# Edge pass of a graph layer: the aggregated row made in one operation, or in two of 512 and 256 columns

## The chip, the cores and the metric

The kernel runs on one core of a Trainium2 chip. A core has five engines with a queue of their own each: TensorE (PE; its weight loads are listed as PEld), VectorE (DVE), ScalarE (ACT), GpSimd (POOL) and SyncE (SP, which here only starts transfers). They are kept in step by semaphores alone: an instruction names a semaphore and the count that it waits for, and another raises the count when it is done. The metric is device time in microseconds, the median of several runs.

## The reference, cut to what matters

A graph attention layer over 50,000 nodes of 768 features and 25,000 edges, followed by a small feed-forward layer:

```python
hv = layernorm(x).reshape(n, 12, 64)
ft = einsum('nhd,od->nho', hv, W)
e  = leaky_relu(a1[src] + a2[dst], 0.2)          # a1, a2: one number per node and head
alpha = segment_softmax(e, dst)
msg = alpha[:, :, None] * ft[src]
agg = segment_sum(msg, dst)
x   = x + relu(agg + einsum('nhd,od->nho', hv, W_res))
x   = x + ffn(layernorm(x))                      # 768 -> 96 -> 768, other weights for six rows
```

The edges are sorted by target node, and everything is fp32.

## The kernel before, in words

The kernel has two passes. The **edge pass** goes over the edges in 196 chunks of 128 (an edge to a partition), and writes for each chunk the sums of its messages by target, 128 rows of 768 columns, to a scratch in memory. The **node pass** goes over the 392 tiles of 128 nodes, gathers those sums and does the rest. The change is in the edge pass alone.

The edge pass is a software pipeline written out by hand. One loop body holds 14 steps, and in each step every engine works on chunks of several ages: a stage that lags the gather by L steps handles chunk c - L in step c. Steps 0 to 27 and the drain are written out; the rest is a hardware loop. Seven chunks make a group: the softmax over the targets, and the small vectors of mean and variance, are worked out once in a group. Each engine's order is the order of the code; nothing moves an instruction.

What matters here, by line. VectorE, in the order of one step:

- L1196 `nm_s`, once in seven steps: the mean times the reciprocal deviation of a group of source rows. ScalarE's L736, which normalizes those rows, waits for it.
- L1213: copies 13 numbers per partition (`a2_all`) that TensorE's small matmul L967 made; not in four of fourteen steps (`OFF_PE`).
- L1231, **the aggregated row**: adds to the masked sum, which TensorE left in PSUM (`sum_ps`, 768 columns in two banks), a rank-one correction (`csr` times a number per partition, `nmd`), and writes the row to one of seven buffers, `agg_ring`. It raises `s_eo`.
- L1249: the messages of a later chunk (768 columns), then L1099 (two statistics of 384 columns each), L1306 (the 0/1 mask of a chunk) and, in some steps, L1330, L1339 and the chain of the softmax (L1312 to L1382).

TensorE, in a step: transposes L904, feature products L913, the small products L941, then the **masked sum** of a chunk: L955 (columns 0 to 511) and L957 (columns 512 to 767) with the mask as weights, and after it L967. An fp32 matmul shows as two loads and two matmuls in the trace. There is one `sum_ps`, so the sum of a chunk may overwrite it only when the row of the chunk before has been made: this is the wait for `s_eo` ahead of L955. In the drain two places take turns (`twice`).

ScalarE, in a step: L736 (normalizes), L762 (copies the transposes out of PSUM), L768 (copies the features), L773 (copies the small products; TensorE's L967 waits for it) and L781 (squares). SyncE starts the store of a row (L515) when `s_eo` has reached its count. VectorE's `nmd` (L1348) and TensorE's work after the pass wait for `s_eo` too.

Of the kernel before, what the change touches and what calls it, by code (L numbers as in the profile page):

```python
# [14 lines left out]
P = 128  # L15
NC = D // P
# [10 lines left out]
G = 7  # L27
BODY = 2 * G
EC = -(-N_EDGES // (P * BODY)) * BODY
# [17 lines left out]
AR = 7  # L47
# [80 lines left out]
def at_least(eng, sem, value):  # L128

    if not isinstance(value, int) or value > 0:  # L130
        eng.wait_ge(sem, value)


def gnn_ffn_kernel(nc, x, x_cols, edges, dst_rows, dst_next, dst_prev, dst_ends, chunk_base, sel_heads,
# [4 lines left out]
    ALU = mybir.AluOpType  # L139
# [4 lines left out]
    with ExitStack() as ctx:  # L144
# [88 lines left out]
        csr = sb("csr", [P, P])  # L233
# [19 lines left out]
        nmd = sb("nmd", [P, 2, G])  # L253
# [40 lines left out]
        with ExitStack() as edge:  # L294
            agg_ring = edge.enter_context(nc.sbuf_tensor("agg_ring", [P, AR, D], f32))
# [7 lines left out]
        def sums(b, co):  # L303

            return sum2_ps if isinstance(b, int) and co > EC - L_SUM + L_FT and (EC - 1 - co) % 2 == 1 else sum_ps

        def twice(b, co):

            return 1 if isinstance(b, int) and co > EC - L_SUM + L_FT + 1 else 0
# [81 lines left out]
        s_eo = sem("s_eo")  # L391
# [73 lines left out]
        def _(sp):  # L465
# [37 lines left out]
            for b in turns(sp, NB, 2):  # L503
                for i in range(BODY):
                    for h, (at, lo, hi) in enumerate(((19, 0, 4), (22, 4, G))):
                        gl = 2 * b + (i - at) // G
                        if (i - at) % G == 0 and exists(gl, NG):
                            at_least(sp, s_mask, G * (gl - 1) + hi)
                            sp.dma_start(dst_all[:, lo * P:hi * P], dst_rows[ds(gl, 1), lo * P:hi * P].to_broadcast([P, (hi - lo) * P]))\
                                .then_inc(d_dst[h], 16)  # L510
                    co_ = BODY * b + i - L_AGG
                    if exists(co_, EC):
                        v = (i - L_AGG) % AR
                        sp.wait_ge(s_eo, co_ + 1)
                        sp.dma_start(agg_v[ds(co_, 1)].rearrange("a p d -> p (a d)"), agg_ring[:, v, :])\  # L515
                            .then_inc(d_agg[v], 16)
                    if isinstance(b, int) and co_ == EC - 12:
                        sp.wait_ge(s_a2c, EC)
                        sp.wait_ge(s_sqd, EC)
                        sp.wait_ge(s_tr, NBLK * EC)  # L520
                        sp.wait_ge(s_ag, EC)
                        sp.dma_start(sel_sb, sel_heads).then_inc(l_fix, 16)
                        sp.wait_ge(d_scat_first, 16 * BODY)
                        sp.wait_ge(d_scat[0], 16 * (EC // 2 - G))
                        sp.wait_ge(d_scat[1], 16 * (EC // 2 - G))
                    if isinstance(b, int) and EC - 12 <= co_ < EC - 12 + EX // PAIR:
                        load_x(PAIR * (co_ - EC + 12), co_ - EC + 12)
                        load_rows(PAIR * (co_ - EC + 12), co_ - EC + 12)
                    if isinstance(b, int) and EC - 7 <= co_ < EC - 7 + EG:
                        load_xt(co_ - EC + 7, co_ - EC + 7)  # L530
# [6 lines left out]
            for b in turns(sp, NT // U, 1):  # L537
                for u in range(U):
                    t = b * U + u
                    if u % PAIR == 0 and exists(t, NT) and not (isinstance(t, int) and t < EX):  # L540
                        v = u % XR
# [30 lines left out]
                    if (u - L_ST) % PAIR == 1 and exists(to, NT):  # L572
                        v = (u - L_ST) % XR - 1
                        sp.wait_ge(s_o, to + 1)
                        settle(sp)
                        lo = NCLS // PAIR if isinstance(b, int) and to == 1 else 0
# [294 lines left out]
        def _(pe):  # L871
# [18 lines left out]
            for b in turns(pe, NB, 2):  # L890
                for i in range(BODY):
                    c = BODY * b + i
                    ct = c - L_TR
                    if exists(ct, EC):
                        v = (i - L_TR) % BODY
# [12 lines left out]
                    if exists(cf, EC):  # L908
                        v = (i - L_FT) % 2
# [14 lines left out]
                    if (i - 19) % G == 0 and exists(gt_, NG):  # L924
                        w = (i - 19) // G % 2
# [10 lines left out]
                    if exists(cf, EC) and (i - L_FT) % BODY not in OFF_PE:  # L936
                        v = (i - L_FT) % 2
# [8 lines left out]
                    co_ = c - L_SUM  # L946
                    if exists(co_, EC):
                        v = (i - L_SUM) % BODY
                        pe.wait_ge(s_msg, co_ + 1)
                        pe.wait_ge(s_mask, co_ + 1)  # L950
                        at_least(pe, s_eo, co_ - twice(b, co_))
                        if isinstance(b, int) and co_ == EC - L_SUM + L_FT + 1:
                            pe.wait_ge(s_eft, EC)
                        to = sums(b, co_)
                        nc.tensor.matmul(to[:, 0:4 * P].rearrange("p (a f) -> p a f", f=P), mask_ring[:, v % 2, :],  # L955
                                         ft_ring[:, v, 0:4, 0:P], start=True, stop=True)
                        nc.tensor.matmul(to[:, 4 * P:D].rearrange("p (a f) -> p a f", f=P), mask_ring[:, v % 2, :],  # L957
                                         ft_ring[:, v, 4:NC, 0:P], start=True, stop=True).then_inc(s_sum, 1)
                    if isinstance(b, int) and c == L_TR:
# [21 lines left out]

            pe.wait_ge(s_coef, 1)
            pe.wait_ge(l_fix, 48)
            pe.wait_ge(s_eo, EC)
            for j in range(NC):
                last = nc.tensor.matmul(ps[:, 3 + j // 2, j % 2 * EC:(j % 2 + 1) * EC], sel_sb[:, j * P:(j + 1) * P],
                                        coef[:, 0, :], start=True, stop=True)
# [21 lines left out]
            for b in turns(pe, NT // U, 1):  # L1009
                for u in range(U):  # L1010
# [7 lines left out]
                    if exists(tu, NT):  # L1018
                        q = b * (U // PAIR) + (u - L_UP) // PAIR
                        v, k = (u - L_UP) // PAIR % 2, (u - L_UP) % PAIR  # L1020
# [10 lines left out]
                    if exists(td, NT):  # L1031
                        v = (u - L_DOWN) // PAIR % 2
                        f = slice((u - L_DOWN) % PAIR * P, ((u - L_DOWN) % PAIR + 1) * P)
# [39 lines left out]
                    if isinstance(t, int) and NT + C_DOWN <= t < NT + C_DOWN + 2:  # L1073
# [3 lines left out]
                        lo, hi = ((0, 512), (512, D))[t - NT - C_DOWN]  # L1077
# [7 lines left out]
        def _(dve):  # L1085
# [8 lines left out]
            V = nc.vector  # L1094
# [71 lines left out]
            for b in turns(dve, NB, 2):  # L1166
                for i in range(BODY):
                    c = BODY * b + i
# [3 lines left out]
                    if k == 3 and exists(gc, NG):  # L1172
                        w = (i - 17) // G % 2
# [7 lines left out]
                    if k == 0 and exists(gv, NG):  # L1181
                        w = (i - 7) // G % 2
# [9 lines left out]
                    if k == 1 and exists(gn, NG):  # L1192
                        w = (i - 8) // G % 2
# [14 lines left out]
                    if exists(c2, EC):  # L1208
                        v = (i - L_SQD) % BODY
                        w, j = v // G, v % G  # L1210
# [13 lines left out]
                    ca = c - L_AGG  # L1224
                    if exists(ca, EC):
                        v = (i - L_AGG) % BODY
                        w, j = v // G, v % G
                        dve.wait_ge(s_sum, ca + 1)
                        dve.wait_ge(s_nmd, 2 * b + (i - L_AGG) // G + 1)
                        at_least(dve, d_agg[v % AR], 16 * (BODY // AR * b + (i - L_AGG) // AR))  # L1230
                        V.scalar_tensor_tensor(agg_ring[:, v % AR, :].rearrange("p (c f) -> p c f", f=P),  # L1231
                                               csr[:, None, :].to_broadcast([P, NC, P]), nmd[:, w, j:j + 1],
                                               sums(b, ca).rearrange("p (c f) -> p c f", f=P), ALU.mult, ALU.add)\
                            .then_inc(s_eo, 1)

                    gd = 2 * b + (i - L_VD) // G
                    if (i - L_VD) % G == 0 and exists(gd, NG):
                        w = (i - L_VD) // G % 2
# [4 lines left out]
                    if exists(cm, EC):  # L1243
                        v = (i - L_MSG) % BODY
                        w, j = v // G, v % G
# [55 lines left out]
                    if exists(cd, EC):  # L1301
                        v = (i - L_DT) % BODY
                        w, j = v // G, v % G
# [10 lines left out]
                    if (i - 21) % G == 0 and exists(ga, NG):  # L1314
                        w = (i - 21) // G % 2
# [10 lines left out]
                    if exists(cr, EC) and (i - L_FT) % BODY in OFF_PE:  # L1326
                        v = (i - L_FT) % BODY
                        w, j = v // G, v % G
# [6 lines left out]
                    if exists(cp, EC) and (i - L_TR) % BODY in OFF_PE:  # L1335
                        v = (i - L_TR) % BODY
                        w, j = v // G, v % G
# [4 lines left out]
                    if (i - L_VD) % G == 0 and exists(gd, NG):  # L1342
                        w = (i - L_VD) // G % 2
                        dve.wait_ge(s_rpd, gd + 1)
                        dve.wait_ge(s_a2c, G * (gd + 1))
                        dve.wait_ge(s_eft, G * (gd + 1))
                        at_least(dve, s_eo, G * (gd - 1))
                        V.tensor_tensor(nmd[:, w, :], a2_all[:, w, :, HEADS], r_d[:, w, :], ALU.mult).then_inc(s_nmd, 1)  # L1348
                        at_least(dve, s_ert, gd - 1)
                        V.tensor_tensor(e_col[:, w, :].rearrange("p (g h) -> p g h", h=HEADS), a2_all[:, w, :, 0:HEADS],  # L1350
                                        r_d[:, w, :][:, :, None].to_broadcast([P, G, HEADS]), ALU.mult).then_inc(s_e, 1)
                        dve.wait_ge(s_e, 2 * gd + 1)
                        e_v = e_col[:, w, :].rearrange("p (g n h) -> p g n h", g=G, h=HC)
                        V.tensor_tensor(e_v, e_v, ft_ring[:, w * G:(w + 1) * G, :, P:FTW], ALU.add).then_inc(s_e, 1)
                        dve.wait_ge(s_e, 2 * gd + 2)
                        V.scalar_tensor_tensor(e_col[:, w, :], e_col[:, w, :], SLOPE, e_col[:, w, :], ALU.mult, ALU.max)\
                            .then_inc(s_leak, 1)
# [65 lines left out]
            for b in turns(dve, NT // U, 1):  # L1423
                for u in range(U):
                    t = b * U + u
                    to = t - L_OUT
                    if exists(to, NT):
                        v = (u - L_OUT) % XR
# [7 lines left out]
                    if exists(ty, NT):  # L1436
                        v = (u - L_Y) % XR
                        g = (u - L_Y) % GR
                        w = (v // PAIR + 1) % (XR // PAIR)
# [133 lines left out]
```

## Time and profile before

| what | value |
|---|---|
| median of 3 runs | 2710.01 us (2706.36 to 2710.99) |
| the profiled execution | 2709.44 us |
| its span, first to last instruction | 2707.6 us |
| TensorE, VectorE, ScalarE busy over the span | 95%, 91%, 87% |
| granted TensorE clock, mean over the span | 0.989 |
| first and last aggregated row | 97.9 us, 1027.7 us |

The times of instructions come from the one profiled execution; the median is over runs of its own. In an answer by time, a row has the start, the duration, the engine, the line of the code, the operation and what it writes and reads; in brackets stands how long the engine was idle before it and what ended that. Rows of equal instructions are merged (x2). `ps` is PSUM, and `arena` is one large area of SBUF that many buffers share, so the line tells more than the name. "issue" means that the engine waited for nothing that the profile shows. Waits for several semaphores are put down to the one that came last.

### The profile page before, as it was taken

The page shows a single profiled execution, that of the slowest core. Times are in us where ns is not written, and L with a number is a line of the kernel's source. Part 1 is how long each engine was busy: PE and PEld are TensorE (multiplying, and loading weights), DVE is VectorE, ACT ScalarE, POOL GpSimd, SP SyncE. Part 2 cuts the span into 40 slices and gives each one's busy share as a digit, 9 for nine tenths or more (in the row PEclk, how much of TensorE's full clock was granted, in tenths as well). Part 3 has the DMA queues.
Part 4 walks back from the last instruction along what each step waited for, and adds up shares of the span by engine and source line. Part 5 has one row for each costly group of instructions (what it writes and reads, how often), then busy time and mean ns, then how long its engine had stood idle before and what let it go on. Part 6 is the DMA issues. An engine that isn't in the chain of part 4 may idle for free. (4 is left out here: it accounts for less than half of the span.)

```text
span 2707.6 us, 67374 instructions
## 1 busy us (share of the span) xinstructions
PE 2564.6 (95%) x20334; PEld 2316.8 (86%) x20334; DVE 2473.7 (91%) x4949; ACT 2362.5 (87%) x4748; POOL 2156.7 (80%) x2029
## 2 busy tenths in 40 slices
PE   5899999999999985999999999999999999999998
PEld 4777777777777754999999999999999999999997
DVE  5799999999999976999999999999999999999996
ACT  5888888888888863999999999999999999999993
POOL 7877777777777616888888888888888888888882
PEclk9999999999999996999999999999999999999999
DMA  8787787887787656899999999999999999999983
GB/s 313 225 258 254 254 257 256 254 255 254 255 258 257 210 182 236 320 348 337 339 331 329 321 329 321 322 320 319 317 315 317 317 315 315 314 311 315 310 312 119
DMA packets 254176, 777.85 MB, mean 287 GB/s; under 512 B 77185, under 2 KB 85165, under 8 KB 253837
## 3 DMA queue, kind: packets, MB, share of 16 engines
q1 hardware_dynamic: 184190, 563.88, 58.8%
q0 software_dynamic: 69312, 210.37, 25.5%
q8 instruction: 121, 1.98, 0.3%
q14 instruction: 121, 0.99, 0.1%
q10 hardware_dynamic: 432, 0.62, 0.1%
HBM read 638.86 MB, written 236.65 MB: 323 GB/s over the span
## 5 line engine op out<-in xcount | busy, mean ns | idle before, releaser
L1051 PE MATMUL ps<-wr_bd,arena 128*128 128x128 f32 x4704 | 593.6, 276 | 18.9 <-DVE arena L1451 18.9
L1051 PEld LDWEIGHTS ps<-wr_bd,arena 128*128 128x128 f32 x4704 | 563.6, 193 | 20.0 <-issue 19.9
L717 POOL DMA_INDIRECT arena<-agg_scratch,nrow x392 | 439.4, 1121 | 76.3 <-issue 66.9
L659 POOL TENSOR_SCALAR arena<-csr_neg,mv,r_n 128x768 f32<-128x768 f32 x392 | 389.9, 995 | 51.0 <-PE ps L887 37.3
L1446 DVE SCALAR_TENSOR_TENSOR ps<-ps,r_n,arena 128x768 f32<-128x768 f32 x392 | 399.1, 1018 | 17.0 <-DMA arena<-agg_scratch,nrow 15.3
L837 ACT ACTIVATE t_hi<-ps 128x768 fp32r<-128x768 f32 x392 | 315.1, 804 | 93.6 <-PE ps L887 93.6
L846 ACT ACTIVATE arena<-arena,s_st 128x768 f32<-128x768 f32 x392 | 364.1, 929 | 29.9 <-DVE arena L1451 29.9
L1451 DVE SCALAR_TENSOR_TENSOR arena<-ps,arena 128x768 f32<-128x768 f32 x392 | 375.4, 958 | 13.4
L707 POOL TENSOR_SCALAR arena<-arena,nm_n,r_n 128x768 f32<-128x768 f32 x392 | 384.7, 982 | 2.6 <-issue 1.8
L1458 DVE TENSOR_TENSOR t_lo<-ps,t_hi 128x768 fp32r<-128x768 f32 x392 | 373.6, 953 | 11.8 <-ACT t_hi L837 11.8
L805 ACT ACTIVATE arena<-arena,mv 128x768 f32<-128x768 f32 x392 | 368.1, 939 | 12.7
L1434 DVE TENSOR_TENSOR arena<-arena,ps 128x768 f32<-128x768 f32 x392 | 369.9, 944 | 5.9 <-PE ps L1042 5.8
L1026 PE MATMUL ps<-t_hi,w_hi 128*96 128x256 f32 x1176 | 361.6, 308 | 0.0
L1026 PE MATMUL ps<-t_hi,w_lo 128*96 128x256 f32 x1176 | 330.0, 281 | 0.0
L887 PE MATMUL ps<-ident,arena 128*128 128x128 f32 x2352 | 323.4, 274 | 6.6 <-POOL arena L707 5.9
L1026 PE MATMUL ps<-t_lo,w_hi 128*96 128x256 f32 x1176 | 329.1, 280 | 0.0
L798 ACT ACTIVATE arena<-arena 128x768 f32<-128x768 f32 x392 | 326.2, 832 | 1.0 <-ACT arena L805 0.4
L653 POOL TENSOR_TENSOR r_n<-ve_n,half 128x4 f32<-128x4 f32 x200 | 209.3, 1047 | 123.1 <-DVE ve_n L1156 122.3
L913 PE MATMUL ps<-wgv,arena 128*128 128x130 f32 x2352 | 295.8, 275 | 0.3
L736 ACT ACTIVATE arena<-arena,nm_s,r_s 128x768 f32<-128x768 f32 x196 | 202.0, 1031 | 90.9 <-DVE nm_s L1196 90.9
L913 PEld LDWEIGHTS ps<-wgv,arena 128*128 128x128 f32 x2352 | 278.8, 191 | 0.7 <-issue 0.7
L887 PEld LDWEIGHTS ps<-ident,arena 128*128 128x128 f32 x2352 | 270.8, 142 | 8.7 <-POOL arena L707 7.9
(226 smaller groups left out, 6248.4 us busy)
## 6 DMA issues: line engine op xcount, KB each, us to landing
arena<-in_x SPq DMA_DIRECT2D x196, 768.0 KB
arena<-in_x_cols SPq DMA_DIRECT2D x392, 384.0 KB, 4.9
out<-arena SPq DMA_DIRECT2D x195, 768.0 KB, 5.6
agg_scratch<-agg_ring SPq DMA_DIRECT2D x196, 384.0 KB, 2.9
dst_all<-in_dst_rows SPq DMA_DIRECT2D x28, 256.0 KB
arena<-agg_scratch,nrow POOLq DMA_INDIRECT x392
arena<-in_x,e_slot POOLq DMA_INDIRECT x364, 4.7
dst_all<-in_dst_rows SPq DMA_DIRECT2D x28, 192.0 KB, 4.4
```

What stands on the lines that cost most here:

```text
L659: pool.tensor_scalar(g_ring[:, g, :].rearrange("p (c f) -> p c f", f=P), csr_neg[:, None, :].to_broadcast([P, NC, P]), mv1[:, w, 2 * (v % ...
L707: pool.tensor_scalar(n2[:, v % 2, :], y_ring[:, v, :], nm_n[:, w, k:k + 1], r_n[:, w, PAIR + k:PAIR + k + 1], ALU.add, ALU.mult).then_inc( ...
L717: pool.indirect_dma_start(g_ring[:, g, :], None, agg_d, bass.IndirectOffsetOnAxis(nrow[:, v, 3:4], 0), bounds_check=EP - 1, oob_is_err=Fal ...
L805: nc.scalar.activation(junk[:, 0, :], x_ring[:, v, :], ACT.Square, bias=mv1[:, w, 2 * k:2 * k + 1], scale=-1.0, accum_out=q_st[:, w, k:k + ...
L887: last = nc.tensor.transpose(dst[:, c * P:(c + 1) * P], src[:, c * P:(c + 1) * P], ident[:])
L913: last = nc.tensor.matmul(ft_ps[:, n // 3, n % 3, :], both_t[:, v, n * P:(n + 1) * P], wgv[:, n, :], start=True, stop=True)
L1026: last = nc.tensor.matmul(ps[0:HID, 6 + v, 0:PAIR * P], w[:, i, :], h[:, i, :], start=(i == 0 and n == 0), stop=(i == NC - 1 and n == 2))
L1051: last = nc.tensor.matmul(res_ps(b, tr)[:, i * P:(i + 1) * P], xt_ring[:, g, i * P:(i + 1) * P], wr_bd[:], start=True, stop=True)
L1434: V.tensor_tensor(y_ring[:, v, :], y_ring[:, v, :], down_ps(b, to), ALU.add).then_inc(s_o, 1)
L1446: V.scalar_tensor_tensor(z, z, r_n[:, w, k:k + 1], g_ring[:, g, :], ALU.mult, ALU.add).then_inc(s_z1, 1)
L1451: V.scalar_tensor_tensor(y_ring[:, v, :], z, 0.0, x_ring[:, v, :], ALU.max, ALU.add, accum_out=s_st[:, w5, k:k + 1]).then_inc(s_y, 1)
L1458: V.tensor_tensor(t2_lo[:, v, :, f], pair(0).rearrange("p (c n) -> p c n", c=NC), t2_hi[:, v, :, f].bitcast(f32), ALU.subtract).then_inc(s ...
```

## The change

The operation of line 1231 becomes a loop of two: columns 0 to 511, and columns 512 to 767. Each raises `s_eo`, so every count of that semaphore is doubled wherever it is waited for. Ahead of the masked sum's first matmul TensorE waits for the first part of the row before (2n - 1 for n rows), and ahead of the second matmul for the second part (2n). Nothing else is changed.

```diff
--- before.py
+++ after.py
@@ -511,7 +511,7 @@
                     co_ = BODY * b + i - L_AGG
                     if exists(co_, EC):
                         v = (i - L_AGG) % AR
-                        sp.wait_ge(s_eo, co_ + 1)
+                        sp.wait_ge(s_eo, 2 * co_ + 2)
                         sp.dma_start(agg_v[ds(co_, 1)].rearrange("a p d -> p (a d)"), agg_ring[:, v, :])\
                             .then_inc(d_agg[v], 16)
                     if isinstance(b, int) and co_ == EC - 12:
@@ -948,12 +948,13 @@
                         v = (i - L_SUM) % BODY
                         pe.wait_ge(s_msg, co_ + 1)
                         pe.wait_ge(s_mask, co_ + 1)
-                        at_least(pe, s_eo, co_ - twice(b, co_))
+                        at_least(pe, s_eo, 2 * (co_ - twice(b, co_)) - 1)
                         if isinstance(b, int) and co_ == EC - L_SUM + L_FT + 1:
                             pe.wait_ge(s_eft, EC)
                         to = sums(b, co_)
                         nc.tensor.matmul(to[:, 0:4 * P].rearrange("p (a f) -> p a f", f=P), mask_ring[:, v % 2, :],
                                          ft_ring[:, v, 0:4, 0:P], start=True, stop=True)
+                        at_least(pe, s_eo, 2 * (co_ - twice(b, co_)))
                         nc.tensor.matmul(to[:, 4 * P:D].rearrange("p (a f) -> p a f", f=P), mask_ring[:, v % 2, :],
                                          ft_ring[:, v, 4:NC, 0:P], start=True, stop=True).then_inc(s_sum, 1)
                     if isinstance(b, int) and c == L_TR:
@@ -981,7 +982,7 @@
 
             pe.wait_ge(s_coef, 1)
             pe.wait_ge(l_fix, 48)
-            pe.wait_ge(s_eo, EC)
+            pe.wait_ge(s_eo, 2 * EC)
             for j in range(NC):
                 last = nc.tensor.matmul(ps[:, 3 + j // 2, j % 2 * EC:(j % 2 + 1) * EC], sel_sb[:, j * P:(j + 1) * P],
                                         coef[:, 0, :], start=True, stop=True)
@@ -1228,10 +1229,12 @@
                         dve.wait_ge(s_sum, ca + 1)
                         dve.wait_ge(s_nmd, 2 * b + (i - L_AGG) // G + 1)
                         at_least(dve, d_agg[v % AR], 16 * (BODY // AR * b + (i - L_AGG) // AR))
-                        V.scalar_tensor_tensor(agg_ring[:, v % AR, :].rearrange("p (c f) -> p c f", f=P),
-                                               csr[:, None, :].to_broadcast([P, NC, P]), nmd[:, w, j:j + 1],
-                                               sums(b, ca).rearrange("p (c f) -> p c f", f=P), ALU.mult, ALU.add)\
-                            .then_inc(s_eo, 1)
+                        for lo, hi in ((0, 4), (4, NC)):
+                            cols = slice(lo * P, hi * P)
+                            V.scalar_tensor_tensor(agg_ring[:, v % AR, cols].rearrange("p (c f) -> p c f", f=P),
+                                                   csr[:, None, :].to_broadcast([P, hi - lo, P]), nmd[:, w, j:j + 1],
+                                                   sums(b, ca)[:, cols].rearrange("p (c f) -> p c f", f=P), ALU.mult, ALU.add)\
+                                .then_inc(s_eo, 1)
 
                     gd = 2 * b + (i - L_VD) // G
                     if (i - L_VD) % G == 0 and exists(gd, NG):
@@ -1344,7 +1347,7 @@
                         dve.wait_ge(s_rpd, gd + 1)
                         dve.wait_ge(s_a2c, G * (gd + 1))
                         dve.wait_ge(s_eft, G * (gd + 1))
-                        at_least(dve, s_eo, G * (gd - 1))
+                        at_least(dve, s_eo, 2 * G * (gd - 1))
                         V.tensor_tensor(nmd[:, w, :], a2_all[:, w, :, HEADS], r_d[:, w, :], ALU.mult).then_inc(s_nmd, 1)
                         at_least(dve, s_ert, gd - 1)
                         V.tensor_tensor(e_col[:, w, :].rearrange("p (g h) -> p g h", h=HEADS), a2_all[:, w, :, 0:HEADS],
```

VectorE's queue in one step of the loop, before, from the copy of the small numbers (L1213) to the statistics; behind each row stand the semaphores it waits for:

```order
L1213 COPY a_all<-ps 128x13 [waits s_sct]
L1231 SCALAR_TENSOR_TENSOR agg_ring<-csr,nmd,ps 128x768 [waits d_agg0,s_nmd,s_sum]
L1246 REGISTER_ALU
L1249 TENSOR_TENSOR arena<-arena,alpha 128x6x128 [waits s_alpha,s_eft]
L1099 BN_STATS bn_a<-arena 128x6 [waits d_gs3]
L1099 BN_STATS bn_a<-arena 128x6
```

The same place after:

```order
L1214 COPY a_all<-ps 128x13 [waits s_sct]
L1234 SCALAR_TENSOR_TENSOR agg_ring<-csr,nmd,ps 128x512 [waits d_agg0,s_nmd,s_sum]
L1234 SCALAR_TENSOR_TENSOR agg_ring<-csr,nmd,ps 128x256
L1249 REGISTER_ALU
L1252 TENSOR_TENSOR arena<-arena,alpha 128x6x128 [waits s_alpha,s_eft]
L1100 BN_STATS bn_a<-arena 128x6 [waits d_gs3]
L1100 BN_STATS bn_a<-arena 128x6
```

The row of 768 columns has become two in a row; the second waits for nothing. The same lines of code stand one to three numbers higher now.

TensorE's queue in one step of the loop, before, from the small products (L941) to the small matmul (L967):

```order
L941 MATMUL ps<-arena 32x128 [waits s_etr]
L941 MATMUL ps<-arena 32x128 x5
L949 REGISTER_ALU
L955 MATMUL ps<-arena 128x512 [waits s_eo,s_mask,s_msg]
L957 MATMUL ps<-arena 128x256
L964 REGISTER_ALU
L967 MATMUL ps<-arena 128x13 [waits s_esc]
```

The same place after:

```order
L941 MATMUL ps<-arena 32x128 [waits s_etr]
L941 MATMUL ps<-arena 32x128 x5
L949 REGISTER_ALU
L131 ISA [waits s_mask,s_msg]
L955 MATMUL ps<-arena 128x512 [waits s_eo]
L958 MATMUL ps<-arena 128x256 [waits s_eo]
L965 REGISTER_ALU
L968 MATMUL ps<-arena 128x13 [waits s_esc]
```

The two matmuls each wait for `s_eo` now; one instruction that works out a register (L131 ISA) has come in ahead of them, and the waits for mask and messages stand at it. The other three engines keep their instructions; only the counts that SyncE waits for are worked out in another way.

## Rows read from the trace of the kernel before

**Rows 1.** The page: span; busy time, share, instructions by engine.

```profile
span 2707.6 us, 67374 instructions
...
PE 2564.6 (95%) x20334; PEld 2316.8 (86%) x20334; DVE 2473.7 (91%) x4949; ACT 2362.5 (87%) x4748; POOL 2156.7 (80%) x2029
```

**Rows 2.** Stretch, length, busy PE, PEld, DVE, ACT, POOL; clock, DMA share, GB/s.

```profile
100.00:900.00 800.00, 753.67 (x6031) 605.65 (x6031) 731.52 (x1729) 692.40 (x1334) 613.66 (x538) 1.00 0.80 256
```

**Rows 3.** Waits, 100 to 900 us: total us, times, longest us.

```profile
ACT arena L736 <- DVE nm_s L1196: 58.6, 23, 2.9
...
PE ps L955 <- DVE agg_ring L1231: 43.1, 46, 1.4
...
DVE a_all L1213 <- PE ps L967: 35.3, 24, 1.5
...
PEld ps L967 <- ACT arena L773: 18.5, 46, 0.5
```

**Rows 4.** Line 1231 over the span: ns min/median/max, first and last start.

```profile
L1231 DVE SCALAR_TENSOR_TENSOR agg_ring<-csr,nmd,ps x196: 995/1005/1017, 97.9 to 1027.7; 128x768 f32<-128x768 f32 x196
```

**Rows 5.** VectorE in order of time: start, us, instruction, idle before.

```profile
500.76 0.16 DVE L1196 SCALAR_TENSOR_TENSOR nm_s<-mvs,r_s 128x7 f32<-128x7 f32 x1
...
501.00 1.01 DVE L1231 SCALAR_TENSOR_TENSOR agg_ring<-csr,nmd,ps 128x768 f32<-128x768 f32 x1
...
501.93 0.95 DVE L1249 TENSOR_TENSOR arena<-arena,alpha 128x768 f32<-128x768 f32 x1
...
502.79 1.01 DVE L1099 BATCH_NORM_STATS2 bn_a<-arena 128x6 f32<-128x384 f32 x2
...
513.66 0.17 DVE L1213 COPY a_all<-ps 128x13 f32<-128x13 f32 x1 [1.47 <-PE ps L967]
...
513.77 1.01 DVE L1231 SCALAR_TENSOR_TENSOR agg_ring<-csr,nmd,ps 128x768 f32<-128x768 f32 x1
...
518.87 1.00 DVE L1231 SCALAR_TENSOR_TENSOR agg_ring<-csr,nmd,ps 128x768 f32<-128x768 f32 x1
...
524.82 1.00 DVE L1231 SCALAR_TENSOR_TENSOR agg_ring<-csr,nmd,ps 128x768 f32<-128x768 f32 x1
...
529.98 1.02 DVE L1231 SCALAR_TENSOR_TENSOR agg_ring<-csr,nmd,ps 128x768 f32<-128x768 f32 x1
...
535.40 0.15 DVE L1196 SCALAR_TENSOR_TENSOR nm_s<-mvs,r_s 128x7 f32<-128x7 f32 x1
```

**Rows 6.** ScalarE in the same stretch.

```profile
500.96 1.03 ACT L736 ACTIVATE arena<-arena,nm_s,r_s 128x768 f32<-128x768 f32 x1 [2.18 <-DVE nm_s L1196]
...
508.00 0.30 ACT L773 ACTIVATE arena<-ps 96x128 f32<-96x128 f32 x1
```

**Rows 7.** TensorE matmuls in the same stretch.

```profile
502.16 1.10 PE L955 MATMUL ps<-arena 128*128 128x512 f32 x2 [1.04 <-DVE agg_ring L1231]
...
508.35 0.39 PE L967 MATMUL ps<-arena 96*128 96x13 f32 x2
...
513.34 0.29 PE L967 MATMUL ps<-arena 96*128 96x13 f32 x2
```

**Rows 8.** TensorE weight loads in the same stretch.

```profile
508.34 0.30 PEld L967 LDWEIGHTS ps<-arena 96*128 96x128 f32 x2 [0.35 <-ACT arena L773]
...
511.94 0.30 PEld L955 LDWEIGHTS ps<-arena 128*128 128x128 f32 x2 [0.20 <-issue]
...
512.48 0.19 PEld L957 LDWEIGHTS ps<-arena 128*128 128x128 f32 x1 [0.24 <-issue]
```

**Rows 9.** Three VectorE groups, 100 to 900 us: busy us, mean ns, idle.

```profile
L1099 DVE BATCH_NORM_STATS2 bn_a<-arena 128x6 f32<-128x384 f32 x328 | 165.9, 547 | 0.0
...
L1249 DVE TENSOR_TENSOR arena<-arena,alpha 128x768 f32<-128x768 f32 x163 | 155.0, 951 | 0.0
...
L1350 DVE TENSOR_TENSOR e_col<-a_all,r_d 128x84 f32<-128x84 f32 x24 | 5.7, 238 | 0.0
```

**Rows 10.** VectorE where the pass drains.

```profile
953.19 0.17 DVE L1213 COPY a_all<-ps 128x13 f32<-128x13 f32 x1 [2.72 <-PE ps L967]
```

## The prediction

> **What bounds the kernel now.** I read the page's busy times first, then the stretch in which the changed lines run, then who waits for whom there, and last the instructions of one group of seven chunks, engine by engine.
>
> The page gives 95% for TensorE and 91% for VectorE over the span [rows 1]; such shares can't tell which engine a stage waits for, and the edit touches only the edge pass. The aggregated rows are made from 97.9 us on, 196 of them, 1005 ns each [rows 4]. In 100 to 900 us VectorE is busy 731.52 of 800 us, TensorE 753.67, ScalarE 692.40 [rows 2]: all three near the top, each with gaps. So this stage is a ring of hand-overs, and the question is which ring closes last. The waits there name four [rows 3]: ScalarE for `nm_s` of VectorE (58.6 us, 23 times), VectorE for the small matmul L967 (35.3 us, 24 times), TensorE's masked sum L955 for the aggregated row (43.1 us, 46 times), and the weight load of L967 for ScalarE's copy L773 (18.5 us, 46 times). 800 us hold 23 groups of 34.6 us, so the first two occur once in each group, the others twice.
>
> Now one group, from `nm_s` at 500.76 to `nm_s` at 535.40 us, which is 34.64 us [rows 5]. ScalarE stood idle 2.18 us for the first `nm_s` and starts at 500.96; up to its copy L773 (508.00 to 508.30) its rows show no idle bracket [rows 6]. TensorE's L967 waits for that copy: its weights load at 508.34 after 0.35 us of idleness [rows 8]. From there TensorE has no idle time up to the next L967 at 513.34 [rows 7]. VectorE, idle for 1.47 us, is released by it at 513.66 and then waits for no other engine up to `nm_s` at 535.40 [rows 5]. That closes the ring: 0.2 us hand-over, 7.3 us ScalarE, 5.3 us TensorE, 21.9 us VectorE, together 34.7 us, the length of the group. The reader should see that four aggregated rows lie on VectorE's part of it (513.77, 518.87, 524.82, 529.98), and that the one at 501.00, for which TensorE's sum waited 1.04 us until 502.16 [rows 7], lies beside it: `nm_s` stands in front of that row in VectorE's order, so ScalarE starts without it.
>
> **What the change does, part by part.**
>
> *The split of the row.* Each of the 196 operations of 768 columns becomes one of 512 and one of 256. Per column VectorE takes (951 - 238) / (768 - 84) = 1.042 ns [rows 9], so 768 columns are 800 ns. From the start of a row to the start of the next instruction there are 501.93 - 501.00 = 0.93 us [rows 5]: 0.13 us beyond its columns, which the split pays once more. The trace has no split row, so this is bounded on both sides. Below: two 384-column statistics in a row take 1.01 us [rows 5] where one takes 547 ns [rows 9], so the second adds 0.463 us, 0.063 more than its 0.400 us of columns; those read no PSUM and no scalar from memory. Above: the whole fixed part of the duration, 1005 - 800 = 205 ns, if nothing of two neighbours overlaps. Less than nothing it can't be, since the columns and their rate stay. I take 0.13 us, as it is this operation's own figure.
>
> How many count? The pattern holds from the first row at 97.9 us to the drain of the pass, where VectorE begins to wait 2.72 us for L967 (953.19 us, [rows 10]) and is no longer the long part. That is 855 / 34.64 = 24.7 groups, so 4 x 24.7 = 99 rows on the ring: 99 x 0.13 = 12.9 us. By the bounds it is 6.2 and 20.3 us. The other three rows of each group add 3 x 0.13 = 0.39 us in front of VectorE's idle 1.47 us [rows 5], and in the drain the idle time is 2.7 us: nothing there. If that cover were gone, all 196 would count, 25 us.
>
> The Trainium skill ("VectorE: DVE Perf Modes", on the TRN2 errata) has a rule that speaks against the change: each VectorE instruction pays a fixed latency between instructions, once, however few columns it has; it fits an fp32 two-tensor operation by (N + 151) / 0.96 ns. This trace agrees on the duration: 919 / 0.96 = 957 ns against 951 in [rows 9]. By that figure every added operation would cost 157 ns, and 99 of them 15.6 us. The same page ("The DRAIN you can't avoid") lets no next operation start before the pipe is empty, which by [rows 9] and [rows 5] would be nearer 0.2 us; here the next row starts at 501.93, 0.08 us before the 1.01 us from 501.00 are over, so I stay with the distance of starts.
>
> *The earlier release.* With 1.042 ns a column the first part takes 1005 - 267 = 738 ns, so TensorE may start a sum 0.27 us earlier. Where it waits, twice a group, that time shows on TensorE. But on the ring it buys nothing: at 508.35 TensorE then waits the longer for ScalarE's copy, which hangs on `nm_s`. The other wait of the group sits inside VectorE's long part, where TensorE's lead is used up again by the next row. I value it at 0; the outer bound is below, as the first rival.
>
> *The second wait.* The second part would end 0.93 - 0.267 + 0.471 = 1.13 us after the first one's start, 0.40 us behind the first part's end. The sum's second weight load comes 512.48 - 511.94 = 0.54 us after its first [rows 8], which itself starts a little after the release. So it finds its count reached, with about 0.14 us or more to spare: 0. What is queued behind it is L967 and the next transposes, which would be late by what is missing.
>
> *Register work.* TensorE's queue gains one register instruction ahead of each sum, since the doubled count has to be worked out. Today the sum's first weight load stands 0.20 us behind the one before it, with nothing waited for [rows 8]; that gap holds one register instruction and three waits. One more is an estimate of a quarter of it, 0.05 us; one sum a group lies on TensorE's part of the ring: 24.7 x 0.05 = 1.2 us, between 0 and 4.9. On SyncE the store of a row starts up to 0.13 us later; seven row buffers, each used every 34.64 us, cover that. VectorE's one more register step a group stands ahead of `nmd` while a 768-column operation runs: 0.
>
> The sum: 12.9 + 1.2 = 14.1 us. The profiled execution took 2709.44 us (span 2707.6 us and 1.8 around it), 0.6 under the median of 2710.01. 2709.4 + 14.1 = 2723.5; I say 2723.
>
> **Rivals.**
>
> *Faster: TensorE's waits are the ring.* Those 46 waits in 800 us would each shrink by 0.27 us; over the 24.7 groups 2 x 24.7 x 0.27 = 13.3 us are won, and VectorE's seven extra starts a group (0.91 us) go into its 1.47 us of idleness: 2696. For it: 43.1 us of waiting, and ScalarE's copy makes TensorE late by only about 0.4 us at each L967. Against it: VectorE shows no wait for 21.9 us of each group, and what stands in that part adds up to the length of the group. It decides if VectorE's part had at least 0.52 us of slack in a group; I see none.
>
> *No change.* The second part starts right behind the first, as its operands need no new wait, and costs almost nothing (under 0.05 us); or TensorE's gain just pays for it: 2710. The statistics pair speaks for a cost near it, 0.063 us; against it stands that this operation reads PSUM and a scalar and shows 0.13 us.
>
> *Slower by more.* Two operations on the same banks of PSUM do not overlap at all: 99 x 0.205 = 20.3 us, and the register step costs its full gap of 0.20 us, 4.9 us: 2735 at the end, 2730 without the latter. For it: the durations. Against: every row is now overlapped by its successor by 0.08 us.
>
> *It does not release as it says.* If the second wait stalls the sum's second half by more than the first half has won, the early release is lost. That changes nothing of the forecast, as the release is valued at 0.
>
> **How the numbers follow.** My forecast (the split's starts on the ring) gets 0.63, no change 0.17, faster 0.08, slower by more 0.12. The forecast's own range goes from the pair's 0.063 us (2716) to 0.157 us and the register step (2727). The range for 8 in 10 reaches to no change below and into the dearer case above: 2709 to 2731. A measurement of this kernel can't tell less than about 0.2%, 5.4 us, from no change; the forecast's low end lies just at it. So slower 0.12 + 0.63 x 0.94 = 0.71, same 0.17 + 0.04 = 0.21, faster 0.08.
>
> **What would show it.** Right: the group from `nm_s` to `nm_s` grows from 34.64 to about 35.2 us; the two parts take near 738 and 471 ns and start 0.66 us apart; VectorE's idle time before L1213 shrinks from 1.47 to about 1.1 us while ScalarE's wait for `nm_s` grows by about half a microsecond; TensorE's wait for the aggregated row does not fall in sum. Wrong in the size: the second part starts less than 0.60 us behind the first (it overlaps), or more than 0.7. Wrong in the place: the group keeps its length although VectorE's row takes longer, or becomes shorter; then the ring ran through L955, and TensorE's wait should have dropped by a quarter of a microsecond each time. The second part of the kernel, after the edge pass, must keep its length; if it doesn't, what I see is not this change.

## The result, and the profile after

| | device time, median | runs |
|---|---|---|
| before | 2709.95 us | 2706.36 to 2710.99 |
| after | 2760.09 us | 2758.57 to 2765.13 |

The change makes the kernel slower by 50.1 us: ratio 1.0191, 95% interval 1.0173 to 1.0208. 2723 us were forecast with 2731 as the upper end, so the sign was right, and the size wrong by a factor of 3.6 against the 14.1 us of the sum. The last row of the edge pass starts at 1078.8 us instead of 1027.7 [rows 4]: all of it arises in that pass.

The page of the kernel after: the span, the busy times, which answer to [rows 1], and the line of one of the two queues that bring instructions (packets, MB, share).

```profile
span 2756.8 us, 67714 instructions
...
PE 2582.4 (94%) x20334; PEld 2328.8 (84%) x20334; DVE 2496.8 (91%) x5145; ACT 2363.9 (86%) x4748; POOL 2138.3 (78%) x2029
...
q14 instruction: 176, 1.44, 0.1%
```

The same queue on the page before:

```profile
q14 instruction: 121, 0.99, 0.1%
```

VectorE's busy time grew by 23.1 us (2473.7 before), no more than the split explains (196 x 0.13 = 25). But the instruction queue moved 55 packets and 0.45 MB more. The two parts of a row, 100 to 900 us, by form (busy us, mean ns, idle before):

```profile
L1234 DVE SCALAR_TENSOR_TENSOR agg_ring<-csr,nmd,ps 128x512 f32<-128x512 f32 x154 | 114.2, 741 | 1.6 <-issue 0.3
L1234 DVE SCALAR_TENSOR_TENSOR agg_ring<-csr,nmd,ps 128x256 f32<-128x256 f32 x154 | 72.9, 474 | 0.0
```

738 and 471 ns were expected. In order of time, both parts (merged) and the next instruction:

```profile
524.00 1.13 DVE L1234 SCALAR_TENSOR_TENSOR agg_ring<-csr,nmd,ps 128x512 f32<-128x512 f32 x2
525.05 0.95 DVE L1252 TENSOR_TENSOR arena<-arena,alpha 128x768 f32<-128x768 f32 x1
```

The second part starts 1.13 - 0.474 = 0.66 us behind the first, as expected, and from start to start the row takes 1.05 us instead of 0.93 [rows 5]: the split costs what was forecast. The rest is in one place. VectorE's rows where its loop jumps back to its beginning, once in two groups (called a turn from here on):

```profile
188.32 0.22 DVE L1385 COPY tab<-m_row 84x2 f32 x1
192.23 0.17 DVE L1185 TENSOR_SCALAR ve_s<-mvs 128x7 f32<-128x7 f32 x1 [3.69 <-issue]
192.36 0.17 DVE L1214 COPY a_all<-ps 128x13 f32<-128x13 f32 x1
192.68 1.14 DVE L1234 SCALAR_TENSOR_TENSOR agg_ring<-csr,nmd,ps 128x512 f32<-128x512 f32 x2 [0.15 <-issue]
```

The first is the last instruction of the loop body, `ve_s` the first one. VectorE stands idle for 3.69 us in between, and "issue" says that it waited for nothing that the profile shows: `ve_s` needs VectorE's own work alone. Before, this gap was there too, but small:

```profile
529.04 0.17 DVE L1382 COPY tab<-m_row 84x2 f32 x1
529.54 0.17 DVE L1184 TENSOR_SCALAR ve_s<-mvs 128x7 f32<-128x7 f32 x1 [0.33 <-issue]
```

All turns of the pass, after and then before (idle us in total, times):

```profile
  issue: 40.0, 11
```

```profile
  issue: 3.7, 11
```

The loop runs 12 passes (2 to 13), so it jumps back 11 times. That is 36.3 us more at the turns, and 55 / 11 = 5 packets (41 KB) for each. The packets lie there in time too: from 170 to 930 us the queue moved none before and 54 after. From one turn to the next (189 to 262 us), after:

```profile
q14 instruction: 5, 0.04, 0.2%
```

One of the five falls into the gap itself (189 to 192.23 us). Counted from `ve_s` to `ve_s`, groups without a turn went from 34.2 to 34.67 us, near the 0.52 us forecast; those with one went from 34.3 us to between 37.6 and 39.2. The waits of 100 to 900 us, which answer to [rows 3]:

```profile
ACT arena L736 <- DVE nm_s L1197: 77.1, 22, 4.8
PEld ps L955 <- DVE agg_ring L1234: 73.4, 77, 4.5
...
PE ps L955 <- DVE agg_ring L1234: 56.6, 45, 4.2
...
DVE a_all L1214 <- PE ps L968: 26.8, 23, 1.3
...
PEld ps L958 <- DVE agg_ring L1234: 11.8, 48, 0.4
```

TensorE's wait for the row did not fall; its longest is 4.5 us now, as the other engines wait for VectorE at its turn. Two theories are left. Theory A: VectorE's loop, 295 instructions before and 309 after, has come to lie so that its beginning is no longer at hand when it jumps back, and has to be fetched. Theory B: the split rows and doubled waits themselves make VectorE late there. The Trainium skill ("Runtime: NRT & Kernel Launch", on instruction fetch mechanics) states A's rule: most engines hold two blocks of 256 instructions, and a taken branch to an instruction outside them waits for a fetch.

### The profile page after: what moved, and what is told of

Same layout as the page of the kernel before. It is cut to its first block and busy times, and to the rows that moved or that the text cites. A ratio compares the mean times of both kernels' runs of the same rounds, so it can differ in the third digit from the quotient of the medians.

```text
span 2756.8 us, 67714 instructions
## 1 busy us (share of the span) xinstructions
PE 2582.4 (94%) x20334; PEld 2328.8 (84%) x20334; DVE 2496.8 (91%) x5145; ACT 2363.9 (86%) x4748; POOL 2138.3 (78%) x2029
## 5 line engine op out<-in xcount | busy, mean ns | idle before, releaser
L887 PE MATMUL ps<-ident,arena 128*128 128x128 f32 x2352 | 321.9, 273 | 6.2 <-POOL arena L707 5.5
L736 ACT ACTIVATE arena<-arena,nm_s,r_s 128x768 f32<-128x768 f32 x196 | 202.0, 1031 | 115.1 <-DVE nm_s L1197 115.1
L955 PE MATMUL ps<-arena 128*128 128x512 f32 x392 | 227.9, 664 | 75.6 <-DVE agg_ring L1234 65.0
L904 PE MATMUL ps<-ident,arena 128*128 128x128 f32 x2016 | 264.4, 280 | 19.3 <-DVE arena L1218 13.1
```

Of the source, the lines that this page charges most:

```text
L887: last = nc.tensor.transpose(dst[:, c * P:(c + 1) * P], src[:, c * P:(c + 1) * P], ident[:])
```

## The experiments

"Shifted" means that VectorE's queue has more instructions ahead of the loop: waits for a count that was reached long before. No run changes the arithmetic. All were timed beside the kernel before on the same chip, which took 2709.01 us there, and 2709.72 us beside the two runs whose counts are worked out row by row.

**The changed kernel, its loop in another place.** The edit, ahead of VectorE's loop:

```diff
             dve.wait_ge(s_memset, N_MEMSETS)
+            for _ in range(64):
+                dve.wait_ge(s_memset, N_MEMSETS)
+                settle(dve)
```

> The changed kernel with 63 instructions more in VectorE's queue ahead of the loop (waits for a count reached long before; no arithmetic changes). Theory A (where the loop lies in the instruction blocks): the changed loop, 309 instructions from the 286th on, no longer lies in two blocks of 256, and its first block has to be fetched again at each of the 11 turns; shifted by 63 it lies in two again. Expected: the idle time before ve_s at a turn falls from 3.1 to 4.7 us back to about 0.3 us, the even and odd groups both take 34.7 us, the time is 2721 to 2724 us. Theory B (the split rows or the doubled waits themselves make VectorE late at the turn): 2758 to 2765 us as without the shift.

Measured: 2723.03 us, ratio 1.005 (1.0036 to 1.0064). The turns (idle us in total, times):

```profile
  issue: 3.2, 11
```

and the instruction queue on its page:

```profile
q14 instruction: 122, 1.00, 0.1%
```

So 37 of the 50 us go away by instructions that do nothing, and what stays, 14.0 us above the kernel before, is the split.

**The kernel before, its loop in a worse place.** The same edit in the kernel before, with 24 for 64.

> The kernel before with 23 such waits more ahead of VectorE's loop; row, sums and loop body unchanged (295 instructions). Theory A: the loop now ends in a third block, so each of 11 turns shows 3 to 4.5 us of idle time before ve_s with no split at all; 37 us more, 2740 to 2752 us. Theory B: nothing, 2706 to 2713 us.

Measured: 2761.36 us, ratio 1.0191 (1.0177 to 1.0205): as slow as the changed kernel, with no row split. Its turns and its instruction queue:

```profile
  issue: 43.7, 11
```

```profile
q14 instruction: 176, 1.44, 0.2%
```

A's number was too low. Of the 52.4 us lost, 40.0 are at the turns, and groups without a turn (from `ve_s` to `ve_s`) took 34.9 us rather than 34.2. Of the 12.4 us beside the turns, 6.5 are 22 smaller gaps, two for each turn, in front of a mask where the kernel before shows none:

```profile
196.36 0.29 DVE L1309 TENSOR_SCALAR arena<-dst_all,dst_slot 128x128 f32<-128x128 int32 x1 [0.35 <-issue]
226.08 0.29 DVE L1309 TENSOR_SCALAR arena<-dst_all,dst_slot 128x128 f32<-128x128 int32 x1 [0.26 <-issue]
```

As built, these two masks are instructions 324 and 451 of VectorE's queue, and the instruction queue moved one packet close behind each (between 196 and 199 us, and between 226 and 230). So these gaps may be fetches too, but no run tests that; the other 5.9 us stay open.

**The kernel before, shifted far.** The edit of the first run, in the kernel before.

> The kernel before with 63 such waits more ahead of VectorE's loop. Theory A: the loop begins in the next block and ends in the one behind, two blocks as before; 2706 to 2714 us, 0.3 us at a turn. It is the control of the first run: it prices the added waits, which both theories put at about nothing. If the shift itself cost time, it would show here.

Measured: 2709.29 us, ratio 1.0001 (0.9992 to 1.0010), 3.8 us at 11 turns. The added waits cost nothing; the place alone counts.

**The kernel before, its loop as long as the changed one.** One satisfied wait behind each row:

```diff
                             .then_inc(s_eo, 1)
+                        dve.wait_ge(s_memset, N_MEMSETS)
+                        settle(dve)
```

> The kernel before, the aggregated row in one operation, with one wait for a count reached long before behind each row: the loop gets 14 instructions more and the stretch ahead of it 4, so it lies where the changed kernel's loop lies (286th to 594th instruction). Theory A: the same idle time of 3 to 4.5 us at each turn as in the changed kernel, about 37 us more, 2743 to 2752 us, while the even groups keep 34.2 us. Theory B: 2706 to 2714 us.

Measured: 2750.17 us, ratio 1.0149 (1.0135 to 1.0163). Its turns and its instruction queue:

```profile
  issue: 44.8, 11
```

```profile
q14 instruction: 176, 1.44, 0.1%
```

Most groups without a turn kept 34.16 us. This is the stall of the changed kernel without any split, so B is refuted; the 41.1 us more at the turns are the whole loss (41.2 us).

Where VectorE's loop lies, in instructions of its queue as built:

| kernel | loop from, to | idle at 11 turns |
|---|---|---|
| before | 282, 576 | 3.7 us |
| after | 286, 594 | 40.0 us |
| after, shifted | 349, 657 | 3.2 us |
| before, shifted little | 305, 599 | 43.7 us |
| before, shifted far | 345, 639 | 3.8 us |
| before, longer loop | 286, 594 | 44.8 us |

One set of edges 256 apart fits all six: one between 577 and 594, the next one lower between 321 and 338. Loops that stall cross both, the others one. Edges 128 apart fit as well: loops that stall then cross three, the others two. The packets of 8 KB, five for a turn and spread in time, and the two gaps 127 instructions apart in the run above speak for the shorter distance; no run decides between the two.

The other runs test the ring of the prediction. All have the 64 waits of the first run ahead of VectorE's loop, which in none of them shows the stall (121 or 122 packets). The diffs below leave those waits out.

**`nm_s` earlier.** The block that makes `nm_s`, moved in the kernel before from the front of step 1 of a group to step 0:

```diff
-                    gn = 2 * b + (i - 8) // G
-                    if k == 1 and exists(gn, NG):
...
+                    gn = 2 * b + (i - 7) // G
+                    if k == 0 and exists(gn, NG):
...
                     if (i - 19) % G == 0 and exists(gm, NG):
                         dve.wait_ge(s_ert, gm + 1)
```

> The kernel before, with nm_s moved in VectorE's order from the front of one step to the step ahead of it, behind the mask and in front of the reciprocal, some 2.3 us earlier; and 63 satisfied waits ahead of the loop, as in the third run, so that the loop lies well. The ring of the prediction (nm_s, ScalarE, L967, VectorE) gets 2.3 us shorter; if it is what closes last, the next ring takes over: row, masked sum L955, TensorE's steps, L967, VectorE. By the 0.35 us (0.1 us, if the matmul array's own end counts) that TensorE waited for ScalarE at L967, that one is 0.1 to 0.35 us shorter: 2700 to 2707 us, with ScalarE's wait for nm_s nearly gone. If the ring never ran through nm_s: 2709 us as in the third run.

Measured: 2702.88 us, ratio 0.9977 (0.9967 to 0.9987): as expected. Its waits, 100 to 900 us:

```profile
PEld ps L967 <- ACT arena L773: 10.4, 23, 0.5
ACT arena L736 <- DVE nm_s L1308: 9.6, 12, 0.9
```

ScalarE's wait for `nm_s` is down from 58.6 to 9.6 us, and yet a group gains only 0.2 us: the path over the row and the masked sum was nearly as long (in the table below, the first sum now starts 3.46 us after `nm_s` instead of 1.39, and L967 9.54 us after it instead of 7.59).

**`nm_s` earlier, all rows split.** Both edits.

> The same earlier nm_s, with every row split as in the changed kernel, shifted. Now the release should count: a group pays four starts of 0.125 us and about 0.05 us of register work, and wins 0.27 us at the sum that closes the ring. Against the run with nm_s earlier alone: +0.28 us a group, 7 us more, so 2707 to 2714 us; if the release still buys nothing, 14 us more than that run, as in the shifted changed kernel.

Measured: 2715.02 us, 12.1 us above `nm_s` earlier alone, between the two expectations: the release buys little.

**Only rows beside the ring split.** The first try:

```diff
-                        for lo, hi in ((0, 4), (4, NC)):
+                        for lo, hi in ((0, 4), (4, NC)) if k in (1, 2, 3) else ((0, NC),):
...
-                                .then_inc(s_eo, 1)
+                                .then_inc(s_eo, 2 if hi - lo == NC else 1)
```

> The changed kernel, shifted, with only three of seven rows split, those in front of which VectorE's idle time of 1.47 us comes (steps 1, 2 and 3 of a group); the other four are one operation that raises the count by two. If the ring holds four rows and not these three: groups near 34.2 us plus the register work, 2709 to 2711 us. If every split row costs the same wherever it stands: 3/7 of 14 us, 2715 us.

Measured: 2716.69 us, ratio 1.0030 (1.0020 to 1.0041), which looked like the other theory. But its loop had 309 instructions, 8 more than the split calls for, as many as there are unsplit rows in it; and 0.04 to 0.07 us were lost in front of each unsplit row on the ring. So it was run again with every operation raising the count by one and the waits' values counted out row by row (`SPLIT` holds the split places, `PER_G` is 7 and their number):

```diff
-                        at_least(pe, s_eo, 2 * (co_ - twice(b, co_)) - 1)
+                        at_least(pe, s_eo, parts(b, i, 1 - twice(b, co_)) - is_split(i, -twice(b, co_)))
...
+def parts(b, i, n):
+    r = i - L_AGG + n
+    return 2 * PER_G * b + PER_G * (r // G) + sum(1 + (m in SPLIT) for m in range(r % G))
```

> The run with three of seven rows split, once more, with counts that give an unsplit row one increment: there, raising the count by two had put one more instruction behind each unsplit row, and VectorE's rows show 0.04 to 0.07 us lost at each of them on its part of the ring. Without that: VectorE's part of a group back at about 21.4 us, groups at 34.25 us, 2707 to 2711 us, if split rows beside the ring cost nothing. If each costs its 0.13 us wherever it stands: 3/7 of 14 us more, 2715 us.

Measured: 2708.83 us, ratio 0.9997 (0.9988 to 1.0006). VectorE in order of time (start, us, instruction, idle before):

```profile
509.42 1.14 DVE L1253 SCALAR_TENSOR_TENSOR agg_ring<-csr,nmd,ps 128x512 f32<-128x512 f32 x2
...
514.09 0.17 DVE L1233 COPY a_all<-ps 128x13 f32<-128x13 f32 x1 [1.17 <-PE ps L984]
514.21 1.01 DVE L1253 SCALAR_TENSOR_TENSOR agg_ring<-csr,nmd,ps 128x768 f32<-128x768 f32 x1
```

Three split rows a group cost nothing there; VectorE's idle 1.47 us has become 1.17.

**`nm_s` earlier, one row of seven split**, first with the count raised by two:

> nm_s earlier, and only the row in step 1 of a group split, the one whose release lets TensorE into its long part; shifted. If the release is worth 0.27 us there once ScalarE no longer stands in front: against nm_s earlier alone 24.7 x 0.27 = 6.7 us less, 2693 to 2701 us, faster than both kernels. If it is worth nothing: as with nm_s earlier alone.

Measured: 2710.11 us, far from the 2693 to 2701 expected, with the same kind of extra instructions (652 - 345 + 1 = 308 in the loop, 296 once they are gone). Then without them:

> nm_s earlier and only the row in step 1 split, with counts that add no instruction. In the run with nm_s earlier and all rows split, the first sum started 0.36 us sooner after nm_s, but the L967 that frees VectorE only 0.15 us sooner, since ScalarE's copy came last again. So against nm_s earlier alone (2702.9 us): 0.15 x 24.7 = 3.7 us less, 2697 to 2701 us. If the release is worth nothing: 2703 us; if the whole 0.36 us: 2694 us.

Measured: 2700.43 us, ratio 0.9967 (0.9955 to 0.9979): faster than both kernels. It is 2.4 us less than `nm_s` earlier alone, where 3.7 were expected; but the two ran on different chips and their intervals overlap (0.9967 to 0.9987 there), so that this difference is not clear of the noise.

The ring, worked out of the traces: means over 18 or 19 groups between 200 and 880 us, in us. A group goes from `nm_s` to `nm_s`; ScalarE's part from the L736 that waits for `nm_s` to the end of the copy L773; VectorE's part from its wait for L967 to `nm_s`. "To first sum" and "to L967" are how long after `nm_s` the first masked sum begins, and the L967 that comes after that copy.

| kernel | group | ScalarE | L967 to L967 | VectorE | to first sum | to L967 |
|---|---|---|---|---|---|---|
| before | 34.28 | 7.34 | 4.98 | 21.39 | 1.39 | 7.59 |
| after, shifted | 34.79 | 7.33 | 4.99 | 21.90 | 1.03 | 7.57 |
| beside the ring, clean | 34.27 | 7.33 | 4.99 | 21.38 | 1.03 | 7.58 |
| `nm_s` earlier | 34.04 | 8.99 | 4.88 | 19.29 | 3.46 | 9.54 |
| earlier, one split, clean | 33.98 | 9.11 | 4.99 | 19.30 | 3.10 | 9.36 |

## Why the prediction was wrong, point by point

- **What bounds the kernel: right.** The ring closes over `nm_s`, ScalarE, L967 and VectorE. With all rows split, only VectorE's part grew (21.39 to 21.90 us), and three split rows beside it cost nothing.
- **The price of the split: right.** 0.13 us from start to start; 0.51 us a group for four rows against 0.52. The shifted changed kernel lies at 2723.03 us, where 2723 was forecast; that this agrees to the microsecond is in part luck, since the sum held 1.2 us of register work that did not show.
- **The earlier release at 0: right in this order.** The first sum starts 0.36 us sooner (0.27 expected), L967 does not (7.57 against 7.59). With `nm_s` out of the way, L967 starts 0.18 us sooner and a group is 0.06 us shorter, which the times of the runs do not show clear of the noise.
- **The second wait: not free.** In the changed kernel the second weight load waited 48 times between 100 and 900 us, 0.25 us on average; the 0.14 us to spare were not there. It cost nothing on the ring, as TensorE's part below shows.
- **Register work on TensorE, 1.2 us: wrong, none shows.** TensorE's part, L967 to L967, takes 4.99 us against 4.98.
- **The step that failed** is the part by part sum. It priced every added instruction by its time on its engine and its place on the ring, and took the pattern of a group to hold "from the first row at 97.9 us to the drain", the loop's turn included. That 4 instructions ahead of the loop and 14 in it move where the loop begins and ends had no term: about 37 us, three quarters of the result. The range left it out too. The profile before had a hint that was not read: every second group `ve_s` stands behind 0.33 us of "issue", right where the loop jumps back.
- **The rivals** all turned on the row, the sums and the waits. The dearer one (2730 to 2735) has the wrong cause: two parts of a row do overlap, 1.13 us together against 0.741 + 0.474 = 1.215.

## What to carry to other kernels

An edit that adds instructions to a long hardware loop can cost more by where the loop then lies than by what they do: look at the idle time before the first instruction of the loop body on every engine, and at the instruction queues' packets, before pricing anything else. Where such a stall shows, shift the loop with instructions that do nothing and measure again, and only then judge the edit. On a ring of hand-overs, an earlier release is worth only the lead over the next longest path, here 0.06 us a group of 0.36.

## What the runs showed of the hardware that was not expected

- A jump back that has to fetch left VectorE idle for 3.1 to 4.7 us in the changed kernel, with 5 packets (41 KB) on the instruction queue for each turn. The rule of the Trainium skill cited above, that such a branch waits for a fetch, agrees with this. The same section of the Trainium skill has the queue refilled in blocks of 16 KiB. That differs from what was measured: packets of 8 KB came one at a time, the first in the gap and the last just before the next turn (one between 258 and 260 us).
- TensorE's granted clock fell after such a stall. The changed kernel (stretch, length, busy times; then clock, DMA share, GB/s):

```profile
187.00:190.00 3.00, 2.78 (x33) 2.57 (x33) 1.36 (x5) 3.00 (x8) 1.24 (x2) 1.00 0.90 286
190.00:193.50 3.50, 0.27 (x10) 0.02 (x1) 1.12 (x4) 1.87 (x5) 0.94 (x1) 1.00 0.09 32
194.00:200.00 6.00, 6.00 (x32) 5.00 (x31) 5.83 (x15) 1.61 (x3) 4.31 (x5) 0.72 0.66 219
200.00:230.00 30.00, 28.83 (x235) 22.90 (x234) 27.85 (x70) 27.65 (x54) 22.28 (x21) 1.00 0.80 259
```

  TensorE was busy 0.27 of 3.5 us, then had 0.72 on average for 6 us, a part of them at 1.2 instead of 2.4 GHz, and the full clock again after that. At the next turn it was the same (0.75 from 266 to 272 us), at the one after not (1.00 from 339 to 345 us). It added nothing that shows: the 36.3 us more at the turns and the split's 14.0 already make 50.3 of 50.1 us.
- Raising a count by two went with one more instruction per operation in VectorE's loop than raising it by one (309 against 301), and with 0.04 to 0.07 us at each on the ring; why, no run shows.
